# Moving the set-up of a channel attention into the last group of the MLP before it

## The reference, cut to what matters

```python
# x: (32, 96, 16, 16) -- 32 images of 96 channels and 256 pixels
x = x + window_attention(layernorm(x))          # 8x8 windows, shifted by 4, 12 heads
x = x + gelu(layernorm(x) @ fc1_w + fc1_b) @ fc2_w + fc2_b      # the MLP, per pixel
# the channel attention, per image
mu, var = mean(x, (1, 2, 3)), var(x, (1, 2, 3))
xn = (x - mu) * rsqrt(var + 1e-5) * ln_g + ln_b
Q, K, V = (depthwise3x3(pointwise(xn, w_p) + b_p, w_d) + b_d for each)   # 8 heads of 12 channels
logits = einsum('bhnc,bhnd->bhcd', K, Q) / alpha
out = V @ softmax(logits)                        # over channels of a head
return einsum('bcij,oc->boij', out, w_f) + b_f + xn
```

## Time and profile before

| | us |
|---|---|
| three runs | 538.63, 542.55, 533.91 |
| median | 538.63 |
| the profiled execution | 542.06 |
| its span (first to last instruction) | 540.4 |

### The profile page before, as it was taken

How to read it: one execution, slowest core, us unless ns; L and a number is a source line. 1 busy time by engine, 2 the same in 40 slices (tenths; PEclk the granted TensorE clock), 3 DMA queues, 4 the chain that set the end, 5 groups by cost and what they waited for, 6 DMA issues and landing times. The chain is left out here.

```text
span 540.4 us, 23612 instructions
## 1 busy us (share of the span) xinstructions
PE 518.1 (96%) x9134; PEld 343.1 (63%) x9134; DVE 365.9 (68%) x1003; ACT 302.1 (56%) x763; POOL 178.3 (33%) x216
## 2 busy tenths in 40 slices
PE   7999999999999999998899999939999999999996
PEld 6777777777777777776674343339655655555553
DVE  1479999999999999997404354436556565656544
ACT  2278877777787778876435563103444444444432
POOL 8433444444434443344200220022433332333300
PEclk8599999999999999999999999957999999999999
DMA  4111111111111101100130132323454434444411
GB/s 83 29 42 32 30 30 46 29 30 30 30 29 24 26 24 29 29 3 2 45 75 21 46 93 71 88 49 79 121 146 124 115 101 118 121 114 105 117 51 32
DMA packets 41177, 32.51 MB, mean 60 GB/s; under 512 B 19240, under 2 KB 36776, under 8 KB 41128
## 3 DMA queue, kind: packets, MB, share of 16 engines
q1 hardware_dynamic: 37544, 26.11, 18.9%
q0 software_dynamic: 3584, 5.72, 4.8%
HBM read 18.36 MB, written 7.13 MB: 47 GB/s over the span
## 5 line engine op out<-in xcount | busy, mean ns | idle before, releaser
L383 POOL TENSOR_TENSOR scores<-scores,peak 128x768 f32<-128x768 f32 x64 | 94.3, 1473 | 135.3 <-DVE peak L552 135.3
L1224 POOL DMA_DIRECT2D x_stack<-padded_x x96 | 52.4, 548 | 97.4 <-PE ps_v L1497 63.4
L446 ACT COPY probs_t<-ps_probs 128x768 f32<-128x768 f32 x64 | 51.1, 799 | 40.7 <-PE ps_probs L706 40.7
L544 DVE TENSOR_TENSOR scores<-ps_scores,bias 128x768 f32<-128x768 f32 x64 | 61.3, 957 | 9.1 <-PE ps_scores L696 7.4
L552 DVE TENSOR_REDUCE peak<-scores 128x12 f32<-128x768 f32 x64 | 61.0, 953 | 2.4
L719 PE MATMUL ps_out<-v_blocks,probs_t 128*64 128x54 f32 x1536 | 57.2, 224 | 1.0 <-ACT out_t L451 0.9
L719 PEld LDWEIGHTS ps_out<-v_blocks,probs_t 128*64 128x64 f32 x1536 | 50.2, 138 | 12.3 <-issue 12.2
L706 PE MATMUL ps_probs<-ident,scores 128*128 128x128 f32 x384 | 55.0, 279 | 0.0
L440 ACT ACTIVATE scores<-scores 128x768 f32<-128x768 f32 x64 | 54.2, 846 | 0.6 <-POOL scores L383 0.6
L1037 ACT ACTIVATE hidden<-ps_hidden,fc_b_folded 128x512 f32<-128x512 f32 x48 | 29.1, 688 | 36.8 <-PE ps_hidden L978 36.8
L1497 PE MATMUL ps_qk<-x_stack,conv_w 40*32 40x256 f32 x1536 | 48.8, 379 | 0.0
(11 more groups left out here) (156 smaller groups left out, 900.2 us busy)
## 6 DMA issues: line engine op xcount, KB each, us to landing
x_stack<-padded_x SPq DMA_DIRECT2D x96, 54.0 KB
x_stack<-padded_x POOLq DMA_DIRECT2D x96, 54.0 KB, 2.7
padded_x<-x_pad SPq DMA_DIRECT2D x32, 121.5 KB, 2.5
x_sliced<-stream SPq DMA_DIRECT2D x48, 64.0 KB, 2.0
mixed<-y_sliced SPq DMA_DIRECT2D x48, 64.0 KB, 2.0
out<-y_sb SPq DMA_DIRECT2D x32, 96.0 KB, 2.0
x_now<-in_x SPq DMA_DIRECT2D x32, 72.0 KB, 1.8
stream<-in_x SPq DMA_DIRECT2D x32, 72.0 KB, 1.9
```

The source lines that it names most:

```text
L383: nc.gpsimd.tensor_tensor(sc, sc, peak[:, par, p, :].unsqueeze(2).to_broadcast((128, HEADS, WN)), ALU.subtract).then_inc(s["shifted"], 1)
L446: nc.scalar.copy(probs_t[:, :], ps_turned).then_inc(s["turned_copied"], 1)
L544: nc.vector.tensor_tensor(scores[:, par, p, :].rearrange("p (g c) -> p g c", g=NG), ps_scores[:, :, 0:GROUP * WN], bias[:, p, :].rearrange ...
L1224: engine.dma_start(x_stack[64 * half + i * HC:64 * half + (i + 1) * HC, slot, :, :], rows).then_inc(landed[slot], 16)
```

## The change

The buffers and semaphores of the set-up move into a class `LastStage`, made before the MLP, and the set-up itself into the MLP's last group:

- Only the moments of images 0 to 15 (groups 0 and 1) are needed at first. PE's first averaging matmul stands before `up(3,1)`, behind a wait for these 16 images' `bn_stats`. The mean chain runs on DVE, the second matmul follows `up(3,1)`, and the transposes of `products` are spread over `up`s and `down`s. DVE takes the eighth moment of group 1 before residual (2,1).
- `products` are made by POOL and not DVE, in memory that `tokens2` used; POOL also zeroes the buffers, behind its work for group 1.
- Images 0 to 5 are normalised by DVE between the residuals of group 3, padded by ACT, and written and, for 0 to 3, gathered by SP between its `join_y`s, and by POOL.
- `x_sliced` has one buffer. `slice_x(g+1, c)` is issued right after `join_y(g, c)`.
- The `bn_stats` of images 24 to 31 move into steps 0 to 2 of the channel attention, and the averages of images 16 to 31 into step 3: one matmul before `gram`, and after it a wait for DVE's mean chain, a second matmul, and then V's convolution.
- In group 0 the two `fill`s of 26 become 15. The `fill`s of the set-up go. The separate constant `eps3` goes; `eps2` is used.

```diff
-    x_sliced = sb("x_sliced", [128, 2, SLICES, CHUNK])
+    x_sliced = sb("x_sliced", [128, SLICES, CHUNK])
...
-        def slice_x(g):
-            need(sp, s["mixed_ready"], (g - 1) * SLICES * 2)
-            for c in range(SLICES):
-                for r in range(QUARTERS):
-                    at = (g * QUARTERS + r) * CHUNK
-                    sp.dma_start(x_sliced[32 * r:32 * r + 32, g % 2, c, :],
-                                 stream[32 * c:32 * c + 32, at:at + CHUNK]).then_inc(x_in[g % 2], 16)
+        def slice_x(g, c):
+            need(sp, s["mixed_ready"], ((g - 1) * SLICES + c + 1) * 2)
+            for r in range(QUARTERS):
+                at = (g * QUARTERS + r) * CHUNK
+                sp.dma_start(x_sliced[32 * r:32 * r + 32, c, :],
+                             stream[32 * c:32 * c + 32, at:at + CHUNK]).then_inc(x_in[g % 2], 16)
...
-        for g in range(GROUPS):
+        for g in range(GROUPS - 1):
             for c in range(SLICES):
                 join_y(g, c)
-            if g + 2 < GROUPS:
-                sp.wait_ge(x_in[g % 2], (g // 2 + 1) * PARTS)
-                slice_x(g + 2)
+                if c == 0 and g > 0:
+                    sp.wait_ge(x_in[(g - 1) % 2], ((g - 1) // 2 + 1) * PARTS)
+                slice_x(g + 1, c)
+        write_padded(sp, last, 0, 0)
+        write_padded(sp, last, 1, 1)
+        join_y(GROUPS - 1, 0)
+        gather_taps(sp, last, 0, 0, 0, 0, last.stacked_sp)
+        write_padded(sp, last, 2, 2)
+        gather_taps(sp, last, 1, 0, 1, 0, last.stacked_sp)
+        join_y(GROUPS - 1, 1)
+        write_padded(sp, last, 3, 3)
+        gather_taps(sp, last, 2, 0, 2, 0, last.stacked_sp)
+        join_y(GROUPS - 1, 2)
+        gather_taps(sp, last, 3, 0, 3, 0, last.stacked_sp)
+        write_padded(sp, last, 4, 0)
+        write_padded(sp, last, 5, 1)
...
# PE, in the loop over the groups (more = g + 1 < GROUPS)
             if g == 0:
-                fill(nc, ps_y[0:C, 0, 0:C], average[:, :], 26)
+                fill(nc, ps_y[0:C, 0, 0:C], average[:, :], 15)
...
+            if not more:
+                pe.wait_ge(s["normed_ready"], GROUPS * SLICES)
+                pe.wait_ge(s["moments_ready"], B // 2)
+                nc.tensor.matmul(ps_mean, average[:, :], stats[:, 0:B // 2, 1::3], start=True, stop=True,
+                                 skip_group_check=True).then_inc(last.moments_pe, 1)
             up(g, 1)
...
+            if not more:
+                pe.wait_ge(last.moments_set, 6)
+                nc.tensor.matmul(ps_spread, average[:, :], last.spread2[:, :, :], start=True, stop=True,
+                                 skip_group_check=True).then_inc(last.moments_pe, 1)
+                turn_weights(0)
             if g > 0:
                 down(g - 1, 1)
+            if not more:
+                pe.wait_ge(last.moments_set, 8)
+                turn_weights(1)
             up(g, 2)
...
+            if not more:
+                pe.wait_ge(last.weights_copied, ROUNDS)
+                turn_weights(2)
             if g > 0:
                 down(g - 1, 2)
+            if not more:
+                pe.wait_ge(last.weights_copied, 2 * ROUNDS)
+                nc.tensor.transpose(ps_final, w["final"][:, :], ident[0:C, 0:C]).then_inc(last.weights_turned, 1)
...
# ACT, last group
+            if g + 1 == GROUPS:
+                act.wait_ge(last.zeroed, ZEROED)
+                copy_weights(0, 1)
+                copy_weights(1, 0)
             gelu(g, 2)
+        nc.scalar.preload_act_table_set("natural_log_exp_and_others")
+        image_deviations(nc, act, last, m["eps2"], 0)
+        copy_weights(2, 2)
+        act.wait_ge(last.weights_turned, 4)
+        nc.scalar.copy(last.final_w[:, :], ps_final).then_inc(last.weights_copied, 1)
+        for t in range(FIRST):
+            pad_image(nc, act, last, mixed, t, t // SLOTS, t % SLOTS)
...
# DVE, last group and after it
+            if g > 1:
+                take_moments(g - 2, 7, 8)
+            if g + 1 == GROUPS:
+                first_mean(nc, dve, last, stats, 0, ps_mean)
+                then_spread(nc, dve, last, 0, ps_spread)
             if g > 0:
                 add_residual(g - 1, 1)
-            if g > 1:
-                take_moments(g - 2, 7, 8)
...
+        dve.wait_ge(last.rstd_set, 1)
+        normalise_image(0)
+        normalise_image(1)
         add_residual(GROUPS - 1, 0)
+        normalise_image(2)
+        normalise_image(3)
+        add_residual(GROUPS - 1, 1)
+        normalise_image(4)
+        normalise_image(5)
         take_moments(GROUPS - 2, 0, 8)
-        add_residual(GROUPS - 1, 1)
         add_residual(GROUPS - 1, 2)
-        take_moments(GROUPS - 1, 0, 8)
...
# PE, channel attention: the whole set-up becomes two waits
+        pe.wait_ge(last.weights_copied, 3 * ROUNDS + 1)
+        pe.wait_ge(last.ones_in, 16 * ROUNDS)
...
+            if is_image(t, SLOTS - 1):
+                need(pe, s["shifted"], t)
+                pe.wait_ge(s2["moments_ready"], B)
+                nc.tensor.matmul(ps_mean, average[:, :], stats[:, B // 2:B, 1::3], start=True, stop=True,
+                                 skip_group_check=True).then_inc(last.moments_pe, 1)
             gram(t)
+            if is_image(t, SLOTS - 1):
+                pe.wait_ge(last.moments_set, 8 + 6)
+                nc.tensor.matmul(ps_spread, average[:, :], last.spread2[:, :, :], start=True, stop=True,
+                                 skip_group_check=True).then_inc(last.moments_pe, 1)
             if not past(t + 1):
                 convolve(t + 1, (slot + 1) % SLOTS, 1, ps_v, s["v_ready"])
```

More of the change, by code:

```diff
@@ new lines, in then_spread, with image_deviations @@
+def then_spread(nc, dve, last, half, home):
+    dve.wait_ge(last.moments_pe, half * 2 + 2)
+    nc.vector.tensor_reduce(last.spread2[:, :, 0], home.rearrange("p (t e) -> p t e", e=2), AX_X,
+                            ALU.add).then_inc(last.moments_set, 1)
+    nc.vector.tensor_scalar(last.moments[:, half * B // 2:(half + 1) * B // 2, 1], last.mean[:, :], -1.0, None,
+                            ALU.mult).then_inc(last.moments_set, 1)
+def image_deviations(nc, act, last, eps, half):
+    act.wait_ge(last.moments_set, half * 8 + 7)
+    nc.scalar.activation(last.log_var[:, :], last.spread2[:, :, 0], ACT.Ln, scale=0.5, bias=eps[0:C, 0:1]).then_inc(last.log_set, 1)
+    act.wait_ge(last.log_set, half + 1)
+    nc.scalar.activation(last.moments[:, half * B // 2:(half + 1) * B // 2, 0], last.log_var[:, :], ACT.Exp,
+                         scale=-0.5).then_inc(last.rstd_set, 1)
@@ new lines, in gather_taps @@
+def gather_taps(engine, last, t, lap, slot, half, landed):
+    need(engine, last.v_ready, t - SLOTS + 1)
+    engine.wait_ge(last.written[slot], (lap + 1) * 16)
+    image = last.padded_x[bass.ds(t, 1)]
+    for i in range(SIDE):
+        rows = bass.AP(image.tensor, image.offset + half * TILE_HEADS * HC * PADW * PADW + i * PADW,
+                       [[PADW * PADW, HC], [HC * PADW * PADW, TILE_HEADS], [1, ROWS]])
+        engine.dma_start(last.x_stack[64 * half + i * HC:64 * half + (i + 1) * HC, slot, :, :], rows).then_inc(landed[slot], 16)
@@ L917, in mlp @@
     x_in = [sem("x_in0"), sem("x_in1")]
-    y_out = [sem("y_out0"), sem("y_out1")]
+    y_out = last.joined
+    FIRST = 6
+    ps_mean, ps_spread = ps_turn[0:C, 0, 0:B], ps_turn[0:C, 0, 2 * B:3 * B]
+    ps_weights = [ps_turn[:, (k + 1) % 2, 0:SIDE * C].rearrange("p (j c) -> p j c", j=SIDE) for k in range(3)]
+    ps_final = ps_turn[:, 0, 0:C]
     def tokens_home(k):
@@ L1038, in gelu, with copy_weights @@
                                      bias=fc1_b[:, part:part + 1]).then_inc(s["gelu_ready"], 1)
+        def copy_weights(kind, place):
+            act.wait_ge(last.weights_turned, kind + 1)
+            for half in range(ROUNDS):
+                rows, heads = slice(64 * half, 64 * half + STACK), slice(half * HALF_C, (half + 1) * HALF_C)
+                columns = slice(place * HC, (place + 1) * HC) if kind < 2 else slice(0, HC)
+                nc.scalar.copy(last.conv_w[rows, kind // 2, :, :, columns],
+                               ps_weights[kind][rows, :, heads].rearrange("p j (h c) -> p j h c", c=HC)).then_inc(last.weights_copied, 1)
         for g in range(GROUPS):
@@ L1465, in step @@
             normalise(t)
+            if is_image(t, SLOTS - 1):
+                then_spread(nc, dve, last, 1, ps_spread)
+            for early in range(SLOTS - 1):
+                if is_image(t, early):
+                    measure_images(B - 8 + 3 * early, min(B - 5 + 3 * early, B))
             if not is_image(t, 0):
```

310 lines of the change are left out of this document (140 added, 170 removed).

## The result

| | before | after |
|---|---|---|
| median of four runs, us | 540.19 | 551.11 |
| lowest and highest | 533.91, 542.55 | 550.25, 552.31 |
| span of the profiled execution | 540.4 | 550.6 |
| mean granted clock | 0.963 | 0.944 |

The changed kernel is slower: the ratio is 1.0243 (1.0146 to 1.0341). It has 350 fewer instructions, nearly all of them fills, and PE is busy for 3 us less. I had forecast 542 us, in 532 to 551. A ratio compares only the runs in the faster of the two states that this kernel's executions show, with such runs of the kernel before made beside them (its medians there were 538.64, 535.80 and 535.93 us), so it is not the quotient of the medians printed here.

The account below looks back on a forecast made before the run. PE bounds the last stage, which moves with its first convolution behind a 28.8 us seam. Terms -4.1 (seam and fills), +5.15 (cold start), +2.7 (step 3) sum to +3.8: median 542.4, said as 542 us, range 532 to 551.

Parts of the forecast that it names:

- Fewer fills in group 0: MLP group 0: two fills cut from 26 to 15 calls, no new wait, 3.9 us gained.
- The wait on moments: Before up(3,1): PE idles 5.3 us for 16 images' moments, then half clock for 10.3 us costs 5.15.
- POOL's products: 18 product instructions on POOL from 323.0, ready at 328 or 338.5, PE wants them about 339; no cost.
- SP's queue as the end of the MLP: MLP end: SP issues for 14.6 us to 377.2, first convolution at 378.0, or 374.1 with the fills' gain.
- The last stage begins cold: +5.15 us: First convolutions run at half clock after PE idles some 10 us; +5.15 us, ends 0 and 10.1.
- The moments of step 3: +2.7 us: Between gram(3) and its v convolution PE waits for DVE's mean chain: +2.7 us, ends 2.1 and 2.9.
- rival (b): The 2.7 us stall of step 3 fells the clock once more: plus 5.15, 547 us; chance 0.17.
- Rival (c): Clock comes back late twice, at the first up after the pause and the first convolutions: 555 us; chance 0.13.

Follow-up runs that it names:

- 85 fills: The changed kernel with 85 in place of 10 fills behind the last down of the MLP: 538.63 us, ratio 1.0038 to the kernel before.
- moments later: The changed kernel with the moments' matmuls and weight transposes one or two steps later in the last MLP group: 541.96 us, ratio 1.0114.
- the single buffer: The kernel before with only the change's single x_sliced buffer, slice_x DMAs issued behind the join_y DMAs: 544.12 us, ratio 1.0181.

## Why the prediction was wrong, step by step

- *Fewer fills in group 0*: right. The second and third `up` start 5.5 and 11.0 us behind the first, before 7.4 and 14.8: 3.7 us, and I had 3.9.
- *The wait on moments*: right in place and size. PE idled 5.1 us (I had 5.3), the clock fell, and PE worked for 5.3 us at half clock and not the 10.3 that I had taken. `down(2,2)` ended 83.8 us behind the first `up`; my sum has 86.3.
- *POOL's products*: no cost; they took 4.7 us in all, at the low end of my range, and were ready 12 us early. (The 323.0 at which I had POOL free is the end of the row, not 7; eighteen instructions at 0.8 us from there end at 337.4, not 338.5.)
- *SP's queue as the end of the MLP*: right as to SP, which took 15.9 us for what I put at 14.6. But POOL, not SP, was last at the barrier: SP was through at 369.6, POOL's drain ended at 371.0 (see below). The 0.7 us that I had for drain and barrier has no row behind it; from SP's last issue to the first convolution it was 2.2. First `up` to first convolution: 110.4 predicted, 110.1 measured, with errors of 1 to 3 us either way that cancel. These issues from SP took 0.63 us each, back to back. The Trainium skill's page "DMA: Bandwidth & Descriptors", section "Anatomy of one DMA", gives the sequencer's dispatch as some 50 ns, for a DMA on the GpSimd path; it is no price for SP's whole issue, and I should not have set it against one. POOL's issues took 0.55 us here.
- *The last stage begins cold: +5.15 us*: the failed step. That the stage would begin cold was forecast, and rightly; the length of the cold was taken from the seam, 10.3 us, where PE did mostly fills. Here it was 32.0 us from the first convolution in the changed kernel, and 23.0 to 24.0 in four others. The first four steps lost 14.7 us where I had 5.15: an error of 9.5, which is all of the miss. The 10.1 that I had set as the upper end did not reach it either. That the convolutions as such are the reason is not shown: behind the wait of the fourth step, with PE at the same stage's work, the clock was back after 3.4 and 6.8 us.
- *The moments of step 3: +2.7 us*: 2.35 in the changed kernel. That a fall of the clock can follow, rival (b), is true, though not there: in the run with 85 fills it made this 5.5 us, and in the one with the moments later 3.9.

Rival (c), slower by over 2%, had the right place in its second half, the first convolutions, but I made it depend on both slow stretches lasting long. One was enough. I also gave it 0.13 while a like case, 20.1 us at half clock at the kernel's start with PE at work in all of them, stood in the earlier trace rows. The Trainium skill, "TensorE: Matmul & The Clock Gate", section "The HAM clock gate", has sustained activity release the throttle, and puts the ramp below 1% of a typical kernel's span. Here it was 14.7 us of 550.6, 2.7%, with PE busy for 99.8% of the cold stretch.

## What to carry to other kernels

Before taking out filler work at a pause of PE, look at what clock the real work behind it would get. The length of a cold stretch is not one number: with PE busy it was 5.3 us (`up`, behind the wait for the moments), 10.3 and 9.0 us (mostly fills, in the kernel before and with the single buffer), 20.1 us at the kernel's start, and 23 to 32 us at the head of the last stage. A sum should carry the longest of these as its bound, not the nearest. After any change that moves the end of a stage on one engine, count the fills again: two kernels here lost 9 and 10 us because PE ran out of fills 5 to 6 us ahead of the next stage. And when DMAs from several places are put in one queue, add up its issues as one would for a compute engine.

## What the runs showed of the hardware

- The same convolutions ran at 1.00 for 147 us once the clock was up, and at 0.50 for 23 to 32 us when the stage began cold (five traces), with PE busy in both. Behind a wait of 1.7 us later in the stage the clock was back after 3.4 and 6.8 us (two traces). What keeps it low at the head of the stage (the mix of matmuls, the idle stretch before it), or what ended it, no run here isolates.
- The wait of 1.7 us in the fourth step was followed by a fall in two traces (85 fills; moments later), and waits of 3.3 and 3.7 us ahead of the last `down` in one each; the same 1.7 us in the changed kernel was not, nor was a wait of 2.9 us ahead of the last `down` in three traces.
- POOL's drain at the barrier ended 3.9 us behind the end of its last DMA issue in the changed kernel (4.5 us long, from 366.5), and SP's after 0.1 us. It ended 0.5 us behind the landing of POOL's last DMA (370.50), and 0.5 to 1.0 us behind it in the eight other traces with these issues; SP's had ended 2.3 us ahead of the landing of its own last one (371.85). So in these traces POOL did not reach the barrier before its DMAs had landed, and SP did.
- The stage that was not touched ended, at the first `up`, between 256.5 and 264.4 us in twelve traces, with the clock at half for 3.4 to 20.5 us near its start and in some for another 10 to 14 us. That is about as wide as the spread of the runs of one kernel (533.91 to 542.55), and the reason why steps and offsets were compared here and not only medians.
